# A signal from GpSimd for each quad, and VectorE's block operands in another order, in a graph network's edge sweep

## The reference

```python
msg_in = concatenate([x[src], x[dst], edge_attr])            # one row for each edge
msgs = maximum(msg_in @ mW1 + mb1, 0) @ mW2 + mb2
agg = segment_sum(msgs, dst) / clip(count, 1)
upd = maximum(concatenate([x, agg]) @ uW1 + ub1, 0) @ uW2 + ub2 + x
# layer 1: segment_sum(x[src], dst)
# layer 2: segment_sum(norm[:, None] * (x @ W)[src], dst), norm from the edge weights
# layer 3: segment_sum(x[src] * norm[:, None], dst)
```

## Time and profile before

| | us |
|---|---|
| median of 3 runs | 956.94 |
| lowest, highest | 954.84, 957.54 |
| span of the profiled execution | 958.9 |
| busy: TensorE, VectorE, ScalarE, GpSimd | 853.5, 639.7, 509.8, 518.0 |
| GpSimd's first and last gather of the sweep begin at | 45.2, 619.9 |

### The profile page before, as it was taken

How to read it: one execution, slowest core, us unless ns; L and a number is a source line. 1 busy time by engine, 2 the same in 40 slices (tenths; PEclk the granted TensorE clock), 3 DMA queues, 4 the chain that set the end, 5 groups by cost and what they waited for, 6 DMA issues and landing times.

```text
span 958.9 us, 20995 instructions
## 1 busy us (share of the span) xinstructions
PE 853.5 (89%) x7785; PEld 783.6 (82%) x7785; DVE 639.7 (67%) x1766; ACT 509.8 (53%) x1029; POOL 518.0 (54%) x477
## 2 busy tenths in 40 slices
PE   2445988888998788999999999998999999999997
PEld 2345978888998788899998999977889888888886
DVE  7607998787877877688888889858653311115664
ACT  3413765655766556677777777843443011114863
POOL 4177777777777877777777777753110000023110
PEclk9767999999999999999999999999999999999999
DMA  5672656556765586666566666664246888884500
GB/s 153 179 176 63 180 166 177 161 171 193 209 183 166 155 148 200 170 171 182 165 184 166 172 183 167 176 194 146 69 154 232 317 287 300 299 287 144 161 23 25
DMA packets 117410, 169.14 MB, mean 176 GB/s; under 512 B 17287, under 2 KB 83485, under 8 KB 117306
## 3 DMA queue, kind: packets, MB, share of 16 engines
q1 hardware_dynamic: 99834, 137.67, 45.0%
q0 software_dynamic: 13872, 28.32, 13.4%
q10 hardware_dynamic: 3600, 1.77, 0.6%
HBM read 109.26 MB, written 58.45 MB: 175 GB/s over the span
## 4 chain that ended last, share of the span: by engine, by line
PE 40%; POOL 34%; issue 10%; DMA 10%; DVE 3%; ACT 2%; SPq 1%; ACTq 0%; DVEq 0%
POOL room L766 33%; PE ps L1870 14%; PE ps L1855 14%; DMA room<-p_rows,idx 7%; PE ps L1694 3%; DMA edge_windows<-room 3%; PE ps L1695 2%; PE ps L1839 2%; PE ps L1728 1%; PE ps L1708 1%; PE ps L1639 1%; ACT h L872 1%; POOL pair L766 1%; DMA ST<-in_src 1%; PE ps L1668 1%
## 5 line engine op out<-in xcount | busy, mean ns | idle before, releaser
L766 POOL DMA_INDIRECT room<-p_rows,idx x416 | 440.4, 1059 | 144.6 <-issue 120.1
L1694 PE MATMUL ps<-room,ident 128*128 128x128 f32 x832 | 175.1, 293 | 61.7 <-DMA room<-p_rows,idx 60.1
L1694 PEld LDWEIGHTS ps<-room,ident 128*128 128x128 f32 x832 | 130.9, 198 | 70.7 <-DMA room<-p_rows,idx 50.9
L1728 PE MATMUL ps<-room 128*128 128x100 bf16 x2400 | 169.3, 207 | 0.0
L1695 PE MATMUL ps<-room 128*128 128x128 f32 x832 | 166.0, 282 | 0.0
L1284 DVE TENSOR_TENSOR room<-room,Wp 128x800 bf16<-128x800 bf16 x300 | 155.4, 572 | 0.0
L903 ACT ACTIVATE g<-ps 128x512 f32<-128x512 f32 x104 | 62.2, 598 | 170.9 <-PE ps L1695 169.4
L1726 PE MATMUL ps<-room 128*128 128x100 bf16 x800 | 151.7, 208 | 0.0
L1728 PEld LDWEIGHTS ps<-room 128*128 128x128 bf16 x2400 | 147.9, 97 | 3.5
L1870 PE MATMUL ps<-room,h 128*128 128x256 f32 (+1 forms) x650 | 136.2, 371 | 0.0
L1870 PEld LDWEIGHTS ps<-room,h 128*128 128x128 f32 x650 | 119.2, 190 | 15.2
(11 more groups left out here) (193 smaller groups left out, 1137.3 us busy)
## 6 DMA issues: line engine op xcount, KB each, us to landing
weight_blocks<-room SPq DMA_DIRECT2D x100, 400.0 KB
room<-weight_blocks SPq DMA_DIRECT2D x12, 3200.0 KB
room<-dst_row SPq DMA_DIRECT2D x104, 128.0 KB
room<-count_blocks SPq DMA_DIRECT2D x8, 1600.0 KB
count_blocks<-room SPq DMA_DIRECT2D x100, 100.0 KB
room<-p_rows,idx POOLq DMA_INDIRECT x416
first_c<-count_blocks SPq DMA_DIRECT2D x4, 1600.0 KB
edge_windows<-room SPq DMA_DIRECT2D x1, 3328.0 KB
```

The source lines that it names most:

```text
L766: return pool.indirect_dma_start(to, None, table, bass.IndirectOffsetOnAxis(ap=at, axis=0))
L1694: pe.matmul(to, ident[:, :], G[:, n % GS, c, :], start=True, stop=False)
L1728: weighed = pe.matmul(bank(6 + hh)[:, at], lo, movw[:, k, a, i, :, t], start=a == 0, stop=a == PARTS - 1)
```

## The change

GpSimd raises a new semaphore `s_turn` once in front of the four gathers of each quad, and VectorE's turn q begins with a wait for q + 3 of these. Inside the turn the work stands in another order: two of the one-hots, two of the weight products, the other two one-hots, `sta`, then the addition, the third product, the `mov` of the next step, and the window copy. A step's operands are made in turn u + 3 (`mov` in turn u + 2), where all were made in turn u + 2. The wait of the products for `mov` becomes a semaphore `s_mov`; two pairs of other semaphores are made one each, with their counts raised.

```diff
@@ GpSimd
                 if q >= GS:
                     pool.wait_ge(s_pre, q - GS + 1)
+                pool.sem_inc(s_turn, 1)
                 for c in range(4):
                     rows_at(G[:, q % GS, c, :], P_tab, idx[:, q, c:c + 1]).then_inc(s_gat[q % GS], 16)
                 if q == 2:
                     pool.wait_ge(s_pst, 16)
-                    pool.wait_ge(s_sidx, 1)
+                    pool.wait_ge(s_sidx, 2)
@@ VectorE
-            def onehot(q):
-                if q >= OS:
+            def onehot(q, cs=range(4)):
+                if q >= OS and cs[0] == 0:
                     dve.wait_ge(s_seg, q - OS + 1)
-                for c in range(4):
+                for c in cs:
                     last = dve.tensor_scalar(oh[:, q % OS, c, :], iota[:, :], dstT[:, q, c:c + 1], None, ALU.is_equal)
-                last.then_inc(s_oh, 1)
+                if cs[-1] == 3:
+                    last.then_inc(s_oh, 1)
...
-            def block_operands(u):
+            def block_places(u):
+
                 if u >= SETS:
                     dve.wait_ge(s_wmm, 2 * (u - SETS + 1))
-                k = u % SETS
-                link(dve.tensor_tensor(mov[:, k, :, :, :],
-                                       iota_k[:, :, :].rearrange("p (a c) t -> p a c t", a=1)
-                                       .to_broadcast([128, NW, KCOLS, 2]), blocks_of(Kt, u, KCOLS), ALU.is_equal))
-                dve.tensor_tensor(sta[:, k, :, :, :],
+                dve.tensor_tensor(mov[:, u % SETS, :, :, :],
+                                  iota_k[:, :, :].rearrange("p (a c) t -> p a c t", a=1)
+                                  .to_broadcast([128, NW, KCOLS, 2]), blocks_of(Kt, u, KCOLS), ALU.is_equal)\
+                    .then_inc(s_mov, 1)
+
+            def block_lo(u):
+                dve.tensor_tensor(sta[:, u % SETS, :, :, :],
                                   iota_l[:, :, :].rearrange("p (a c) t -> p a c t", a=1)
                                   .to_broadcast([128, NW, 128, 2]), blocks_of(LOt, u, 128), ALU.is_equal)
-                for a in range(PARTS):
+
+            def block_weights(u, parts):
+                if parts[0] == 0:
+                    dve.wait_ge(s_mov, u + 1)
+                k = u % SETS
+                for a in parts:
                     last = dve.tensor_tensor(movw[:, k, a, :, :, :], mov[:, k, :, :, :],
                                              blocks_of(Wp[:, a, :], u, KCOLS), ALU.mult)
-                last.then_inc(s_bop, 1)
+                if parts[-1] == PARTS - 1:
+                    last.then_inc(s_bop, 1)
...
             for q in range(NQ + 1):
+                u = q - LAG + 1
+                if q < NQ:
+                    dve.wait_ge(s_turn, min(q + 3, NQ))
+                if q + 1 < NQ:
+                    onehot(q + 1, (0, 1))
+                if 0 <= u < STEPS:
+                    block_weights(u, (0, 1))
+                if q + 1 < NQ:
+                    onehot(q + 1, (2, 3))
+                if 0 <= u < STEPS:
+                    block_lo(u)
                 if q >= 1:
                     add(q - 1)
+                if 0 <= u < STEPS:
+                    block_weights(u, (2,))
+                if 1 <= u + 1 < STEPS:
+                    block_places(u + 1)
+                if q >= 1:
                     if q - 1 + LEAD < NQ:
                         q_window(q - 1 + LEAD)
...
-                if q + 1 < NQ:
-                    onehot(q + 1)
...
                 if q == 2:
                     weight_parts()
                     find_flag()
+                    block_places(0)
...
-                if 0 <= q + 2 - LAG < STEPS:
-                    block_operands(q + 2 - LAG)
                 piece_steps(q)
```

More of the change, by code:

```diff
@@ L308, in gnn_kernel @@
         s_lst = sem("last_dst_stored_then_first_counts_loaded")
-        s_lmm = sem("last_dst_spread")
-        s_nq = sem("quads_before_block")
+        s_lmm = sem("last_dst_spread_then_flag_summed")
+        s_turn = sem("quad_begun_by_pool")
         s_lg = sem("last_dst_gathered")
@@ L313, in gnn_kernel @@
         s_pst = sem("edge_windows_stored")
-        s_sidx = sem("windows_known")
+        s_sidx = sem("quads_before_block_then_windows_known")
         s_win = sem("windows_gathered")
@@ L327, in gnn_kernel @@
         s_whole = sem("edges_counted")
-        s_fmm = sem("flag_summed")
+        s_mov = sem("block_places_ready")
         s_flag = sem("flag_known")
@@ L768, in _ @@
             pool.wait_ge(s_lst, 16)
-            pool.wait_ge(s_nq, 1)
+            pool.wait_ge(s_sidx, 1)
             for g in range(GROUPS):
@@ L1189, in _ @@
             link(dve.tensor_scalar(nq_f[:, :], nq_f[:, :], float(NQ - 1), None, ALU.min))
-            dve.tensor_copy(nq_i[:, :], nq_f[:, :]).then_inc(s_nq, 1)
+            dve.tensor_copy(nq_i[:, :], nq_f[:, :]).then_inc(s_sidx, 1)
             norm(0, 0)(0)
@@ L1314, in find_flag @@
             def find_flag():
-                dve.wait_ge(s_fmm, 1)
+                dve.wait_ge(s_lmm, 2)
                 link(dve.tensor_copy(whole1[:, 0:2], ps[0:1, 512 * 6:512 * 6 + 2]))
@@ L1775, in _ @@
                     pe.wait_ge(s_whole, 1)
-                    pe.matmul(ps[0:1, 512 * 6:512 * 6 + 2], ones, whole[:, :], start=True, stop=True).then_inc(s_fmm, 1)
+                    pe.matmul(ps[0:1, 512 * 6:512 * 6 + 2], ones, whole[:, :], start=True, stop=True).then_inc(s_lmm, 1)
                 if q + 1 < NQ:
```

## The result

The changed kernel takes 988.80 us (median of 4 runs, 984.96 to 989.49), the kernel before 957.22 in the same comparison. The ratio is 1.0326, with a 95% interval of 1.0299 to 1.0353: slower by 31.6 us. The prediction was 958, its range 940 to 968; of its chances 0.39 stood on a gain and 0.28 on a loss. It missed.

A forecast was written before the change was run, and what follows sets the result against it. GpSimd's gather calls, lengthened by VectorE's heavy operations, were taken to pace the sweep, with TensorE limiting gains. 956.9 us plus 1.1 for the new order, with 0 for signal, wait and later operands, gave 958 us; range 940 to 968.

The forecast's parts named there:

- The single record that I had taken for eight: GpSimd's wait of L781, recorded at 49.9 us: eight calls handed over and not yet done, so signals go out early.
- (b) without a held phase: VectorE's new order, calls walked from ten phases: mean loss 0.34 before, 0.36 after; +1.1 us over quads 3 to 56.
- the 0 of the later quads: Second stretch (quads 57 to 103): the new order's difference in call loss is hidden by TensorE's pace.
- its rule: A gather call that finds a heavy VectorE operation running ends 0.82 us after that operation.
- both locks: VectorE's turn stays in bad phases to the calls (964 us, chance 0.28) or in good ones (948 us, 0.13).
- The lock in bad phases: Rival: VectorE's phase stays among the five worst, +7 us, up to +13 with short records; 964 us; chance 0.28.
- its own mark of 0.43 us a quad: Gather-call loss in the first stretch (quads 14 to 56) above which the bad-phase lock is decided.
- covered by TensorE's pace: Quads 57 to 103: TensorE, busy 246.39 of 254.35 us, hides the order's difference; its gather waits are 7.6 us.
- The first rival: Signal goes out with the calls, pinning VectorE's turn to a call; quads of 5.0 us, 941 us; chance 0.26.

The follow-up runs named there:

- e2: Kernel before, in its old order, with only the signal and the wait for q + 3 added: 956.55 us, ratio 1.0000.
- e3: Changed kernel with the wait for q + 6 in place of q + 3, so that it holds VectorE: 986.10 us, ratio 1.0289.
- e5: Changed kernel with the wait for q + 6 and the window copy moved between third product and places: 963.61 us, ratio 1.0072.
- e10: Changed kernel with the wait for q + 6 and the order addition, window copy in two halves, third product, places: 947.39 us, ratio 0.9901.
- e12: Changed kernel, wait for q + 3 kept (not holding), order addition, window copy in two halves, third product, places: 963.81 us, ratio 1.0045.
- e9: Kernel before, old order unchanged, with the signal and a wait for six added: 955.98 us, ratio 0.9998.
- e4: Changed kernel, wait for q + 3 kept (not holding), window copy moved between third product and places: 983.81 us, ratio 1.0294.
- e7: Changed kernel, wait for q + 3 kept (not holding), order addition, window copy, third product, places: 967.41 us, ratio 1.0100.
- e6: Changed kernel with the wait for q + 6 and the order addition, window copy, third product, places: 986.55 us, ratio 1.0288.

## Why the prediction was wrong

**What was right.** GpSimd's calls pace the sweep; the loss sits in them and the dense stages behind don't move. The wait never holds beyond turns 0 and 1, and signal and waits cost nothing (e2). The reason was right in kind, the sequencer runs ahead of its engine. Its size was off: twelve calls, not eight. The Trainium skill (Advanced Engine Details and Errata, Engine Queue Depths) gives GpSimd eight entries; the trace shows twelve here, and the measurement decides. The single record that I had taken for eight lies in the sweep's first five microseconds, before the sequencer had got its full lead: in the changed kernel the signals in front of quads 3, 4, 5 and 6 are out 0, 4, 8 and 12 calls early. In the changed kernel a one-hot follows the window copy without idle time, as forecast.

**The step that failed** is "(b) without a held phase": the walk of the calls through a turn, mean 0.34 to 0.36 us a turn, +1.1 us. What it gave as +1.1 us for quads 3 to 56 measures some 20 us up to quad 56, and the 0 of the later quads measures 8. Less the two long additions (2.2 us each), the first stretch measures (34.8 - 4.4)/43 = 0.71 us a quad and the second 27.8/47 = 0.59. Two things in that walk were wrong.

*A call was charged with one operation only.* Of the changed kernel's excess, 28 calls that waited through two make 24.7 us: 21 through product and places (19.2), 7 through two products (5.5). In the kernel before only the call beside the addition of L1341 did (3.2 us, of which 0.5 for the places); the prediction read it as a wait for one operation, so the row that contradicts its rule stood among its own. Other meetings with a product rose by some 10 us, those with places and L1285 fell by some 7. These sum to the 28.2 us within 2. The second operation by itself makes 13.6 us of the 24.7: with each of the 28 charged for its first only, on the same trace, the growth would be some 15 us. That the places directly behind the product cost the call was tested by putting the copy between them at the same phase: 1.66 us became 1.18 (e3, e5). The walk had moreover put 0.06 us between the product's end and the places; in the trace the places begin before the product ends (269.37 against 269.45).

*The phases were averaged.* The prediction named both locks as rivals and priced them by means over five phases. The lock in bad phases was the side that came true, at 0.28: the loss passed its own mark of 0.43 us a quad. But it was priced at +7 to +13 us, since the changed order's walk, which charges one operation, gives at most 0.61 us a turn. (Its bounds are taken against the measured 0.38 us and its middle against the walk's own 0.34, which makes 2 us and decides nothing.) In the changed kernel itself the lock is partial, short runs of the same meeting. Where the turn is held, it does not visit five phases, it repeats one: 5.75 us a quad in e3, 5.28 in e5, 5.05 in e10, with the same operations in each. e12 against e10 shows with the order untouched that the phase decides.

*The second stretch was covered by TensorE's pace*, so the prediction said. It grew by 8.2 us. TensorE's 246 busy of 254 us left it little room to be faster, but a later gather still made it wait (7.6 to 15.1 us). The cover works in one direction only.

**The first rival** (faster, 941, by a pinned turn) rested on a signal that goes out with the calls, which it does not. With the wait moved by three quads the turn is pinned, and the change as written still gains nothing (e3), since by the rows of e3 the held turn starts 0.23 us before the quad's first call and not with it, so that the third call does not meet the addition but the product behind it. With the order shifted by one operation and 0.06 us the pinned turn gives 947 (e10). The shape of that rival was right and needed two corrections.

**What stays open.** Why a call is passed over at some distances and not at others, and in front of some pairs and not of others. These are counts over the thirteen traces whose operands are whole; a call is counted if the operation that it meets ends more than 0.126 us behind its start, and as having waited through both if its own end lies within 0.06 us of 0.82 behind the second operation.

| operation met, the next directly behind it | call's start behind the operation's start, ns | waited through both |
|---|---|---|
| product, then places | -5 to 25 | 117 of 132 |
| | 25 to 195 | 0 of 65 |
| | 195 to 210 | 42 of 47 |
| | from 210 on | 0 of 81 |
| first of two products, changed orders | -5 to 25 | 2 of 2 |
| | 25 to 140 | 43 of 93 |
| | 140 to 245 | 43 of 49 |
| | from 245 on | 2 of 120 |
| old order (before, e2, e9): places, L1280 and products, one behind another | from 25 on | 0 of 264 |
| product, then copy, addition or one-hot | any | 0 of 474 |

So a run of heavy operations does not by itself make a call wait twice: the old order has five in a row, and no call waited through two of them, though 17 came 25 to 50 ns and 22 came 100 to 140 ns behind a product with another behind it, where the changed orders gave 13 of 17 and 25 of 37. What differs between the two orders there is not shown; in the old one these calls met the second of three products, in the changed ones the first of two, behind one-hots. No experiment here shows the mechanism. Nor was it tried what sets the phase in the unheld kernels; the trace shows runs of turns without idle time on VectorE, as from 268.68 to 273.09 above, in which a meeting repeats.

## What to carry to other kernels

Where one engine's calls are paced by another engine's operations, don't average over phases: look for a pattern that repeats a single meeting, for an edit of order can move the time by tens of microseconds at nearly unchanged busy times of the other engine. Check the costliest row against the rule that you took from the ordinary ones. Where the trace shows calls that wait through two operations, pin the phase with a wait that truly holds, and put an operation that reads PSUM between the two (e5), or tune their position by tens of nanoseconds until no call meets them (e10). Here the second was worth more by 16 us, and neither the pin alone (e3) nor an order alone (e4, e7, e12) was faster than the kernel before. Before relying on a signal raised by a sequencer, measure from its record how many instructions of its engine are still undone.

## What the runs showed of the hardware

- A gather call that starts during a VectorE operation with two SBUF inputs (128x800 or 128x1024, bf16) ends 0.82 us behind it. In the operation's first 0.04 us it can also be let through (0.94 to 0.95 us). With a second such operation directly behind (0.48 us from start to start) it can wait through both, 1.66 to 1.86 us, in the pairs and at the distances of the table above; in e6 one call waited through three operations (5.26 us).
- A few hundredths of a microsecond decide 0.9 us: a product begun 3 ns behind the call's start cost 0.91 us (e6), one begun 62 ns behind it nothing (e10).
- `sem_inc` on GpSimd acts when the sequencer passes it, in 97 of 104 cases with 12 indirect DMAs still undone, some 17 us before the engine gets there in this sweep, and costs nothing that e2 can tell.
